# Graph network kernel: the second layer of the edge networks put one round further back, with a PSUM bank for each of two results

## The reference

```
h = relu(layernorm(x))
x = x + degree-scaled scatter-add over the edges of h[src]
h = relu(layernorm(x))
n = LN(MLP(h));  e = LN(MLP(edge_attr))            # encoders: Linear, SiLU, Linear, LayerNorm
for s in 0, 1:
    e   = e + LN(MLP([e, n[senders], n[receivers]]))   # edge network, 192 -> 64 -> 64
    agg = segment_sum(e, receivers)
    n   = n + LN(MLP([n, agg]))                        # node network, 128 -> 64 -> 64
out = x + MLP(n)
```

## Time and profile before

| what | value |
|---|---|
| three runs | 15863.53, 15900.21, 15902.72 us; median 15900.21 |
| profiled execution | 15783.89 us, its span 15782.1 us |
| mean granted TensorE clock in it | 0.654 of full |
| instructions | 218306 |
| first layer, step 1, step 2 | about 4.9, 5.3, 4.9 ms of the span |

### The profile page before, as it was taken

How to read it: one execution, slowest core, us unless ns; L and a number is a source line. 1 busy time by engine, 2 the same in 40 slices (tenths; PEclk the granted TensorE clock), 3 DMA queues, 4 the chain that set the end, 5 groups by cost and what they waited for, 6 DMA issues and landing times. The chain is left out here.

```text
span 15782.1 us, 218306 instructions
## 1 busy us (share of the span) xinstructions
PE 10472.3 (66%) x65479; PEld 7604.9 (48%) x65479; DVE 5063.8 (32%) x10190; ACT 5416.2 (34%) x8544; POOL 8925.4 (57%) x9488
## 2 busy tenths in 40 slices
PE   5677777777777766666666666665666666666666
PEld 4566666666666534343334444443444334444444
DVE  8522222233333322232223333332222222222223
ACT  0233333333333333333333333333333333333333
POOL 1366666666665555555555555555666666666565
PEclk8655555555555566666667677676666676677776
DMA  2111111111111122222223333332222222222222
GB/s 65 23 30 30 30 30 30 30 36 35 36 35 35 39 68 68 70 70 66 68 68 79 78 78 79 77 79 65 55 56 56 55 56 57 59 58 59 58 59 51
DMA packets 1513872, 857.93 MB, mean 54 GB/s; under 512 B 1044173, under 2 KB 1204574, under 8 KB 1512881
## 3 DMA queue, kind: packets, MB, share of 16 engines
q1 hardware_dynamic: 1115074, 571.64, 13.5%
q0 software_dynamic: 302816, 231.81, 9.2%
q10 hardware_dynamic: 95408, 47.86, 1.1%
HBM read 616.95 MB, written 249.33 MB: 55 GB/s over the span
## 5 line engine op out<-in xcount | busy, mean ns | idle before, releaser
L1802 POOL DMA_INDIRECT edge_blk_g<-sender_part,edge_blk_lst x6256 | 5918.2, 946 | 4380.0 <-issue 1810.9
L1402 POOL DMA_INDIRECT fl_gx<-sender_x,fl_lst x3128 | 2958.7, 946 | 2357.2 <-issue 894.1
L1874 ACT ACT_TABLE_LOAD x1564 | 2006.6, 1283 | 60.3 <-ACTq L966 31.9
L1947 DVE SCALAR_TENSOR_TENSOR agg<-edge_blk_aggps,vecs,agg 64x64 f32 x1564 | 441.9, 283 | 4409.4 <-remote 4162.1
L1837 PE MATMUL edge_blk_yps<-b_parts,one_bf 96*128 96x256 bf16 x1564 | 395.6, 346 | 2127.3 <-ACT edge_blk_h L1888 2046.9
L1858 PEld LDWEIGHTS edge_blk_hps<-ident,edge_blk_g 128*128 128x128 f32 x6256 | 1163.5, 251 | 1331.0 <-issue 1315.9
L1880 ACT ACTIVATE edge_blk_sq<-edge_blk_yps 128x512 f32<-128x512 f32 x782 | 466.9, 597 | 3741.4 <-remote 3209.4
L1841 PE MATMUL edge_blk_yps<-w_edge_blk,edge_blk_h 64*128 64x64 f32 x12512 | 1372.7, 368 | 444.6 <-issue 443.6
L1853 PE MATMUL edge_blk_hps<-edge_blk_oha,edge_blk_win 128*128 128x512 f32 x1564 | 1474.2, 1028 | 254.6 <-issue 238.1
L1858 PE MATMUL edge_blk_hps<-ident,edge_blk_g 128*128 128x128 f32 x6256 | 1192.2, 332 | 594.1 <-issue 573.0
L1841 PEld LDWEIGHTS edge_blk_yps<-w_edge_blk,edge_blk_h 64*128 64x128 f32 x12512 | 1215.8, 273 | 638.4 <-issue 637.5
(11 more groups left out here) (278 smaller groups left out, 12248.4 us busy)
## 6 DMA issues: line engine op xcount, KB each, us to landing
edge_blk_e<-edge_state SPq DMA_DIRECT2D x782, 256.0 KB
edge_state<-fl_e SPq DMA_DIRECT2D x391, 256.0 KB
edge_blk_dlb<-local_dst SPq DMA_DIRECT2D x1564, 64.0 KB
edge_blk_g<-sender_part,edge_blk_lst POOLq DMA_INDIRECT x6256
edge_state<-edge_blk_new SPq DMA_DIRECT2D x391, 256.0 KB
fl_gx<-sender_x,fl_lst POOLq DMA_INDIRECT x3128
edge_blk_win<-receiver_part SPq DMA_DIRECT2D x1564, 16.0 KB
fl_attr<-attr_slots SPq DMA_DIRECT2D x391, 32.0 KB
```

The lines of the kernel that those rows point to most:

```text
L1402: pool.indirect_dma_start(out=gx[n.b][:, j % TILES, j // TILES, D:D + X_DIM], out_offset=None, in_=xg_d, in_offset=bass.IndirectOffsetOnAx ...
L1802: pool.indirect_dma_start(out=g[n.b][:, i, 64 * c:64 * c + 64], out_offset=None, in_=ps_d, in_offset=bass.IndirectOffsetOnAxis(ap=lst[n.b] ...
L1874: nc.scalar.activation(idle[:, k:k + 1], eps_c[:, :], func)
```

## The change

In all three stages TensorE's second layer, ACT's Square and Sqrt and DVE's reduction, reciprocal and t are put one round further back: from n-1 to n-2 in the message steps, from n-2 to n-3 in the first layer. Sums and turn stay at n-3 and n-4. The result y_ps is now one bank for a round and there are two by parity, so the second layer waits for t of two rounds before. The two bias matmuls of 256 columns become one of 512, and the eight matmuls on row halves become four of 128x128 with the block-diagonal `w_mid`. The first layer gets four h buffers where it had two, its TensorE body runs encode first and the second layer behind it, and its ACT body silu first and scale behind it. The idle tile of the table loads has 8 columns in place of 2. The ends of the stages follow.

```diff
@@ -1344,14 +1344,13 @@
         ohb = many(QUAD, "ohb", [P, 8, WIN])
         e = many(QUAD, "e", [P, CHUNK])
         attr_t = many(2, "attr_t", [64, P])
-        h = many(2, "h", [P, CHUNK])
+        h = many(QUAD, "h", [P, CHUNK])
         sq = sb("sq", [P, 8, D])
         red, sd, rs = (sb(k, [P, 8]) for k in ("red", "sd", "rs"))
-        idle = sb("idle", [P, 2])
+        idle = sb("idle", [P, 2 * QUAD])
         at_ps, agg_ps, t_ps, keys = ps("atps"), ps("aggps"), ps("tps"), ps("keys")
         h_ps, n_ps = ps("hps"), ps("nps")
-        y_ps = ctx.enter_context(nc.psum_tensor("fl_yps", [P, 2, 512], F32))
-        y_all = y_ps[:, :, 0:TILES * D]
+        y_ps = [ps(f"yps{i}") for i in range(2)]
...
@@ -1462,8 +1458,8 @@
                     ins.then_inc(turned, 1)
 
                 def body(n, i=None, j=None):
-                    second(n.back(2))
                     encode(n.back(1))
+                    second(n.back(3))
                     turn_in(n)
                     sums(n.back(4))
                     turn(n.back(4))
...
                 def silu(n, i=None, j=None):
                     if not n.exists():
                         return
-                    warm(ACT.Silu)
+                    warm(ACT.Silu, n)
                     wait(act, pre, n)
-                    wait(act, y_ok, n.back(2))
-                    nc.scalar.activation(h[n.half][:, :], h_ps[:, :], ACT.Silu, bias=col("b0")).then_inc(h_ok, 1)
+                    wait(act, y_ok, n.back(4))
+                    nc.scalar.activation(h[n.b][:, :], h_ps[:, :], ACT.Silu, bias=col("b0")).then_inc(h_ok, 1)
                     if i is not None:
                         nodes.act_late_silu(act, i, j)
-                    warm(ACT.Sqrt)
+                    warm(ACT.Sqrt, n)
 
                 def body(n, i=None, j=None):
-                    scale(n.back(2))
+                    silu(n.back(1), i, j)
+                    scale(n.back(3))
                     if i is not None:
                         if i == BEHIND:
                             wait(act, added, n.back(BEHIND))
                         nodes.act_late(act, i, j)
-                    silu(n.back(1), i, j)
-                    if i is not None:
                         nodes.act_late_dma(act, i, j)
...
@@ -1601,7 +1597,7 @@
                 def body(n, i=None, j=None):
                     attr_copy(n)
                     one_hots(n.back(2))
-                    normed(n.back(2))
+                    normed(n.back(3))
                     add_sums(n.back(4))
...
@@ -1731,10 +1727,9 @@
         h = many(2, "h", [P, CHUNK])
         sq = sb("sq", [P, 8, D])
         red, sd, rs = (sb(k, [P, 8]) for k in ("red", "sd", "rs"))
-        idle = sb("idle", [P, 2])
+        idle = sb("idle", [P, 2 * QUAD])
         h_ps = [ps(f"hps{i}") for i in range(2)]
-        y_ps = ctx.enter_context(nc.psum_tensor(tag + "yps", [P, 2, 512], F32))
-        y_all = y_ps[:, :, 0:TILES * D]
+        y_ps = [ps(f"yps{i}") for i in range(2)]
         t_ps, agg_ps, keys, n_ps = ps("tps"), ps("aggps"), ps("keys"), ps("nps")
         nodes = NodeTiles(sem=sem, n_ps=n_ps, more_ps=t_ps, **work)
         list_in, dlb_in, win_in, g_in, e_in, e_out = (
...
@@ -1832,20 +1827,17 @@
                     if not n.exists():
                         return
                     wait(pe, h_ok, n)
-                    wait(pe, t_ok, n.back(1))
-                    for c in range(2):
-                        nc.tensor.matmul(y_ps[:, c, 0:TILES * D], one_bf[:, :], b1_parts[:, 0:TILES * D], start=True, stop=False)
+                    wait(pe, t_ok, n.back(2))
+                    nc.tensor.matmul(y_ps[n.half][:, :], one_bf[:, :], b1_parts, start=True, stop=False)
                     for i in range(TILES):
-                        for c in range(2):
-                            q = slice(64 * c, 64 * c + 64)
-                            ins = nc.tensor.matmul(y_ps[:, c, D * i:D * i + D], h[n.half][q, P * i:P * i + P], w_mid[q, q],
-                                                   start=False, stop=i == TILES - 1)
+                        ins = nc.tensor.matmul(y_ps[n.half][:, P * i:P * i + P], h[n.half][:, P * i:P * i + P], w_mid[:, :],
+                                               start=False, stop=i == TILES - 1)
                     ins.then_inc(y_ok, 1)
 
                 def body(n, i=None, j=None):
                     sums(n.back(3))
                     turn(n.back(3))
-                    second(n.back(1))
+                    second(n.back(2))
                     if i is not None:
                         nodes.pe_late(pe, i, j)
                     landed(pe, win_in, n, 32)
...
-                def warm(func):
-                    k = 0 if func == ACT.Silu else 1
+                def warm(func, n):
+                    k = 2 * n.b + (0 if func == ACT.Silu else 1)
                     nc.scalar.activation(idle[:, k:k + 1], eps_c[:, :], func)
 
                 def scale(n):
                     if not n.exists():
                         return
                     wait(act, y_ok, n)
-                    nc.scalar.activation(sq[:, :, :].rearrange("p (c i) d -> p c (i d)", c=2), y_all, ACT.Square).then_inc(sq_ok, 1)
+                    nc.scalar.activation(sq[:, :, :], y_ps[n.half][:, :].rearrange("p (j d) -> p j d", d=D),
+                                         ACT.Square).then_inc(sq_ok, 1)
                     wait(act, red_ok, n)
                     nc.scalar.activation(sd[:, :], red[:, :], ACT.Sqrt, bias=eps_c[:, 0:1], scale=1.0 / D).then_inc(sd_ok, 1)
 
                 def silu(n, i=None, j=None):
-                    warm(ACT.Silu)
+                    warm(ACT.Silu, n)
                     wait(act, pre, n)
...
                 def body(n, i=None, j=None):
-                    scale(n.back(1))
+                    scale(n.back(2))
...
@@ -1931,8 +1926,8 @@
                     wait(dve, sd_ok, n)
                     v.reciprocal(rs[:, :], sd[:, :]).then_inc(r_ok, 1)
                     wait(dve, r_ok, n)
-                    v.tensor_tensor(t[n.b][:, :, :, :].rearrange("p i c d -> p c i d"), y_all.rearrange("p c (i d) -> p c i d", d=D),
-                                    rs[:, :].rearrange("p (c i d) -> p c i d", c=2, d=1).broadcast_to([P, 2, TILES, D]), ALU.mult).then_inc(t_ok, 1)
+                    v.tensor_tensor(t[n.b][:, :, :, :].rearrange("p i c d -> p (i c) d"), y_ps[n.half][:, :].rearrange("p (j d) -> p j d", d=D),
+                                    rs[:, :].rearrange("p (j d) -> p j d", d=1).broadcast_to([P, 8, D]), ALU.mult).then_inc(t_ok, 1)
 
                 def add_sums(n):
                     if not n.exists():
...
@@ -1958,7 +1953,7 @@
                     one_hots(n)
                     add_sums(n.back(3))
                     finish(n.back(3))
-                    normed(n.back(1))
+                    normed(n.back(2))
                     if i is not None:
                         nodes.dve_late(dve, i, j)
 
```

More of the change, by code:

```diff
@@ L1490, in _ @@
                 pe.wait_ge(s_ld, weights_landed)
-                nc.tensor.matmul(y_ps[:, 0, :][:, 0:NVEC], mean_w[:, :], vecs[:, :], start=True, stop=True).then_inc(s_vm, 1)
+                nc.tensor.matmul(y_ps[0][:, 0:NVEC], mean_w[:, :], vecs[:, :], start=True, stop=True).then_inc(s_vm, 1)
                 pe.wait_ge(s_diag, 1)
                 k = VEC.index("edge_enc")
-                nc.tensor.matmul(y_ps[:, 1, :][:, 0:D], ones_d[:, :], diag[k][:, :], start=True, stop=True).then_inc(s_rows, 1)
+                nc.tensor.matmul(y_ps[1][:, 0:D], ones_d[:, :], diag[k][:, :], start=True, stop=True).then_inc(s_rows, 1)
                 pe.wait_ge(prepared, 1)
                 last = rounds_and_nodes(pe, body, count_sb, 2)
-                second(last.back(2))
                 encode(last.back(1))
+                second(last.back(3))
                 for k in (4, 3, 2, 1):
@@ L1501, in _ @@
                     turn(last.back(k))
-                    if k == 4:
-                        second(last.back(1))
+                    if k > 2:
+                        second(last.back(k - 2))
                 nodes_again(pe, lambda u, j: nodes.pe_whole(pe, u, j), count_sb)
@@ L1542, in _ @@
                 last = rounds_and_nodes(act, body, count_sb, 2)
-                scale(last.back(2))
                 silu(last.back(1))
-                scale(last.back(1))
+                for k in (3, 2, 1):
+                    scale(last.back(k))
                 wait(act, added, last.back(1))
@@ L1693, in _ @@
                 last = rounds_and_nodes(dve, body, count_sb, 2)
[L1694 to L1696 removed]
+                for k in (2, 1, 0):
+                    if k:
+                        one_hots(last.back(k))
+                    normed(last.back(k + 1))
                     add_sums(last.back(k + 2))
                     finish(last.back(k + 2))
[L1699 to L1701 removed]
+                add_sums(last.back(1))
+                finish(last.back(1))
```

(3 more changed lines are left out.)

19 lines of the change are left out of this document (7 added, 12 removed).

## The result

| | us |
|---|---|
| before, 4 runs | 15901.47 median, 15863.53 to 15912.27 |
| changed, 4 runs | 16079.91 median, 16042.46 to 16111.25 |
| changed / before | 1.0119, interval 1.0094 to 1.0144 |
| profiled executions | before 15783.89, changed 16063.03 |

The change makes the kernel 1.2% slower. The time is inside the wide range of 15,300 to 16,300 that was given, outside the forecast's own 15,550 to 15,850, and on the other side of the kernel before: 15,710 was predicted, and 16,080 is near the price of rival C.

The account below looks back on a forecast made before the run. POOL's gather burst, with results seen after it, was taken to bound each round. Terms 0 - 168 - 40 + 0 + 0 + 15 = -193 us on the 15900.2 median gave 15,710; own range 15,550 to 15,850, wide range 15,300 to 16,300.

Parts of the forecast that it names:

- rival C: Step 1: late second-layer result delays new and the index list, rounds take 14.3 us, +262 us, about 16,160; chance 0.32.
- The burst ends the round, and results are seen after it: All stages: TensorE results finished late in POOL's gather burst are seen after it, giving step 2's 12.3 us period.
- The silu wait: Message steps: TensorE's wait for h before the second layer goes; counted 0, low end a gain of 868 us.
- Second-layer matmuls: TensorE's second layer, 18 recorded passes to 9, 1.76 to about 1.57 us a round under the burst: 0.
- In the crawl: Step 1's paired bursts, TensorE slow: fewer records save 1.4 us for each of 120 pairs, -168 us, ends 0 and -234.
- Step 2 and the first layer: These stages have 117 us above the plain period; a third taken as gain, -40 us.
- Two banks: Second bank for y_ps: TensorE waited for t only 13.5 us in step 1's window, so 0.
- The new wait: Sums wait for t with one body of slack, not two: 0, ends 0 and +2.6 us a round (+1017 in step 1).
- First layer: First layer: encode ahead of the second layer, silu ahead of Square; POOL's release keeps its place, so 0.
- The Trainium skill's row tiling rule: Second layer: 64-row contractions can be row-tiled at up to twice the rate, so merging costs up to +2064 us if unhidden.

Follow-up runs that it names:

- first sets: Runs on one slower chip: parts of the change, then the changed kernel with step 1's second layer doubled; the kernel before took 15982.36, later 15756.03 us.
- third set: 13 runs on three other chips, variants of the kernel before and the changed one against the kernel before: ratios 0.9997 to 1.0002, before 12,389 to 12,393 us.
- e2: Merged matmuls and two banks alone in the message steps, second layer unshifted, first layer as before, against the kernel before: 16268.95 us, ratio 1.0184.
- e15: Changed kernel with step 1's second-layer matmuls issued twice, measured against the kernel before on the slower chip: 15745.80 us, ratio 0.9985.
- e3: Kernel before with only the one-round shift in the message steps, old matmuls and one y, first layer as before: 16187.11 us, ratio 1.0135.
- e1: Changed first layer with both message steps as before, against the kernel before: 15877.09 us, ratio 0.9924.
- e10: The changed kernel itself against the kernel before, on a chip where nothing waits: 12386.82 us, ratio 1.0000.

## Why the prediction was wrong, point by point

- *The burst ends the round, and results are seen after it.* Right for the chips of the result and of the first sets, and the whole effect hangs on it. It depends on the chip, not on the program alone, as the third set shows; the trace of before could not tell that.
- *The silu wait: gone, worth 0.* The wait is gone. Right in step 2 (+0.06 us a round).
- *Second-layer matmuls: 0, under the burst.* Their own time was right (1.56 us a round, 1.57 taken). The price was wrong: by themselves, with the second bank (e2), they cost 0.75 us a round of step 1, 293 us. I treated time saved under a cover as worth nothing, while it decides whether the next result is seen in a burst.
- *In the crawl: -168.* **This is the step that failed.** I took the 120 pairs as given and asked only how long each would be. Their number moved: the list waits went from 120 to 168 and from 991.5 to 1528.1 us (by the timelines, the late bursts with another right behind from 86 to 136), and step 1 took 332 us more instead of 168 less. The saving was computed for an earlier TensorE, and an earlier TensorE is what makes pairs (e15 shows it from the other side).
- *Step 2 and the first layer: -40.* Step 2 gave nothing (+23 us by its windows), the first layer 59.
- *Two banks: 0.* Not tried apart from the merge.
- *The new wait: 0, ends 0 and 2.6.* Partly wrong. It came, 1178 and 1281 us of it, and the shift alone (e3) costs 0.35 us a round in step 1 and 0.19 in step 2, nearer the 0 that I took than the 2.6. How much of the changed kernel's loss is its own is open, as the two parts don't add. In step 2, beside the lighter matmuls, it comes to no more than 0.06.
- *First layer: 0.* Wrong on the good side: e1's ratio of 0.9924 is about 120 us (its median is 105 under before). Its windows give 59 us in the changed kernel. Why the reordering gains, no run takes apart.
- *Rival C* had the right stage, chain (new, SP, list, POOL) and price: 16,160 against 16,080. That the price fits is in part luck: it has every round run as the pairs do, with no gain in the first layer. Its trigger, a second layer that runs late behind the shift, is not what makes the larger part: e2 shifts nothing and has the loss. For what e3 adds, it stays possible. Its mechanism was named in my "for" as "a freed TensorE will run further into the next burst", and then not costed.
- *The Trainium skill's row tiling rule* ("TensorEngine Tiling (Array Packing)", When to Use Tiling) would have made the merged form dearer; the trace after agrees with the rows of before and not with it, 1.56 against 1.76 us (in 5600 to 10600 us, where both kernels had a granted clock of 0.69, 500.2/346 = 1.45 against 638.4/366 = 1.74).

## What to carry to other kernels

When a chain closes on itself (result, transfer, next burst), time saved on an engine under cover is not free of effect: ask at which instant its result has to be seen, and what is released if it comes before. In a queue that serves several consumers, issue what the next stage waits for ahead of any wait for a late result: here one load put a round later, on the chip where results are seen late, was worth more than the change had hoped for. Where a kernel's time rests on such late results, measure on more than one chip before a change of 1% is taken or left.

## What was not expected of the hardware

The same program takes 15,756 to 15,982 us on one chip and 12,389 to 12,393 us on three others, with equal busy time on POOL (8.9 ms). On the slower chip a result that TensorE ends in the later part of a burst of indirect gathers is seen only after it (5980.99 seen at 5985.60 in e15); on a faster one silu starts 0.04 us after the matmuls' end (e10). What makes the chips differ, no run here shows. Second, a kernel with one matmul group doubled was faster than the one it came from, by their ratios to before (0.9985 against 1.0119).
